# A phase-mixer layer on one core: square addition by DMA, and another order of the first step

## The reference, cut to what matters

```python
def attn(x):                       # x is the layernorm of the input
    omega = einsum('bsd,ed->bse', x, W_omega) + b_omega
    phi = cumsum(omega * exp(log_scale) / sqrt(position), axis=1)
    cm_real, cm_imag = x * cos(phi), x * sin(phi)
    mem_real = cumsum(cm_real, axis=1) / position
    mem_imag = cumsum(cm_imag, axis=1) / position
    ret_real = mem_real * cos(phi) + mem_imag * sin(phi)
    ret_imag = mem_imag * cos(phi) - mem_real * sin(phi)
    context = concatenate([cm_real, cm_imag, ret_real, ret_imag], -1)
    h = gelu(einsum(layernorm(context) * ln_gamma + ln_beta, W1) + b1)
    return x + einsum(h, W2) + b2
x = x + attn(layernorm(x))
x = x + ffn(layernorm(x))          # relu(x @ q(W1).T + b1) @ q(W2).T + b2
# q(W) = clip(round(W / (mean(abs(W)) + 1e-5)), -1, 1): weights of -1, 0 or 1
```

## Time and profile before

| | |
|---|---|
| median of 3 runs | 1533.1 us (1530.54 to 1534.26) |
| the profiled execution's own time | 1533.96 us |
| its span, first to last instruction | 1532.2 us |
| busy: PE, DVE, ACT, POOL | 1470.5, 1438.2, 1253.4, 616.9 us |
| mean granted clock of PE | 0.991 |
| DMA: moved, mean rate | 158.20 MB, 103 GB/s |

### The profile page before, as it was taken

How to read it: one execution, slowest core, us unless ns; L and a number is a source line. 1 busy time by engine, 2 the same in 40 slices (tenths; PEclk the granted TensorE clock), 3 DMA queues, 4 the chain that set the end, 5 groups by cost and what they waited for, 6 DMA issues and landing times.

```text
span 1532.2 us, 29929 instructions
## 1 busy us (share of the span) xinstructions
PE 1470.5 (96%) x10685; PEld 878.0 (57%) x10685; DVE 1438.2 (94%) x2325; ACT 1253.4 (82%) x1773; POOL 616.9 (40%) x393
## 2 busy tenths in 40 slices
PE   3779999999999999999999999999999999999998
PEld 2445566656555665555665655566565566555556
DVE  7999999999999999999999999999999999989954
ACT  6768888888988888988888898888888788888756
POOL 1333444433354443444444334444344444334331
PEclk9899999999999999999999999999999999999999
DMA  6325545555645655654555564455565455555452
GB/s 219 67 58 111 102 80 109 108 111 113 123 76 100 111 104 111 124 107 79 105 111 110 111 125 94 83 111 103 109 125 109 73 109 111 110 111 101 73 90 42
DMA packets 231427, 158.20 MB, mean 103 GB/s; under 512 B 138608, under 2 KB 221552, under 8 KB 231280
## 3 DMA queue, kind: packets, MB, share of 16 engines
q0 software_dynamic: 59376, 83.37, 34.3%
q1 hardware_dynamic: 170272, 69.25, 18.4%
q10 hardware_dynamic: 1632, 3.67, 0.7%
HBM read 24.13 MB, written 33.03 MB: 37 GB/s over the span
## 4 chain that ended last, share of the span: by engine, by line
DVE 35%; PE 24%; issue 14%; ACT 12%; POOL 7%; DMA 4%; SPq 2%; DVEq 1%; ACTq 0%; POOLq 0%
PE ps L966 11%; DVE arena L1332 5%; POOL sqr L535 4%; DVE arena L1400 4%; PE ps L1000 4%; PE ps L987 4%; POOL sqr L537 3%; PE ps L1021 3%; ACT xs L601 3%; DVE mr L1285 3%; ACT base L581 3%; DVE arena L1361 2%; DVE bn L1170 2%; DVE arena L1356 2%; DVE qb L1316 2%
## 5 line engine op out<-in xcount | busy, mean ns | idle before, releaser
L966 PE MATMUL ps<-arena,w_hi 128*128 128x512 f16 x2048 | 609.2, 379 | 3.0 <-DVE arena L1332 1.6
L966 PE MATMUL ps<-arena,w_lo 128*128 128x512 f16 x1024 | 388.3, 379 | 0.0
L966 PEld LDWEIGHTS ps<-arena,w_hi 128*128 128x128 f16 x2048 | 197.5, 98 | 224.2 <-issue 2.0
L987 PE MATMUL ps<-turned,fw_t 128*128 128x512 f16 x1024 | 250.6, 380 | 8.6 <-DMA turned<-rows 4.1
L1000 PE MATMUL ps<-fw_t,arena 128*128 128x256 f16 x2048 | 255.0, 273 | 1.9 <-DVE arena L1400 1.9
L1000 PEld LDWEIGHTS ps<-fw_t,arena 128*128 128x128 f16 x2048 | 197.8, 97 | 63.8 <-issue 16.7
L704 ACT ACTIVATE arena<-ps,relu_bias,relu_scale 128x512 f32<-128x512 f32 x256 | 197.0, 769 | 24.8 <-PE ps L987 24.4
L535 POOL TENSOR_TENSOR sqr<-sqr,turn 128x1024 f32<-128x1024 f32 x32 | 84.3, 2635 | 323.3 <-DVE arena L1332 323.3
L1400 DVE TENSOR_TENSOR arena<-arena 128x512 f16<-128x512 f32 x256 | 172.0, 681 | 19.5 <-ACT arena L713 17.5
L1021 PE MATMUL ps<-w_hi,arena 128*128 128x256 f16 x1024 | 172.9, 273 | 0.3 <-issue 0.3
L966 PEld LDWEIGHTS ps<-arena,w_lo 128*128 128x128 f16 x1024 | 100.0, 98 | 121.0
(11 more groups left out here) (189 smaller groups left out, 2850.4 us busy)
## 6 DMA issues: line engine op xcount, KB each, us to landing
x_rows<-in_L_attn_x SPq DMA_DIRECT2D x32, 512.0 KB, 6.5
rr<-qa POOLq DMA_DIRECT2D x32, 512.0 KB, 6.2
ri<-qb POOLq DMA_DIRECT2D x32, 512.0 KB, 9.0
base<-bias_rows POOLq DMA_DIRECT2D x32, 512.0 KB, 5.5
x<-bias_rows POOLq DMA_DIRECT2D x32, 512.0 KB, 5.5
out<-x SPq DMA_DIRECT2D x31, 512.0 KB, 7.6
out<-x POOLq DMA_DIRECT2D x31, 512.0 KB, 11.2
arena<-in_L_attn_W ACTq DMA_DIRECT2D x1, 2048.0 KB, 11.8
```

The lines of the kernel that those rows point to most:

```text
L966: last = pe.matmul(ps[:, 4 + m], w[:, k, m * P:(m + 1) * P], a[:, c.b, k], start=(i == 0), stop=(i == len(passes) - 1))
L987: last = pe.matmul(ps[:, 4 + m % KE], fw1_t[:, k, m * P:(m + 1) * P], a[:, k], start=(i == 0), stop=(i == len(passes) - 1))
```

## The change

In every step, POOL's L535 becomes an accumulating DMA that no longer waits for `cl_done[3]` (only the addition behind it does), and `output_sum` is issued ahead of `product_imag_sin`. In the first step POOL's `square_lo` comes ahead of `base_bias`; ACT waits for `prepared` behind `whole_turns`; PE waits at its start for the `W1` halves alone; DVE makes `gelu_lo` ahead of the comparisons of `fw2`; PE issues `omega(far)`, two sign groups, `mixer_out`, and the last two sign groups, in this order. The mixer of chunk 0 writes banks 6 and 7, so `hidden` of chunk 1 waits for each `z_done[m]` and, from m = 2 on, for `x1_done`. On DVE the block of scales (L1637 to L1651) moves behind `context_lo` 1 to 3 and the phase scans of chunk 1.

```diff
+        ps_rows_first = ps[:, 6:8, :].rearrange("p b (t d) -> p (b t) d", d=D)
...
+        def mixer_rows(c):
+
+            if c.index == 0:
+                return ps_rows_first
+            return ps_rows_last if c.index == CHUNKS - 1 else ps_rows_b
...
             def step(s):        # POOL
+                if nxt and not now:
+                    square_lo(nxt, ahead)
                 if ahead:
                     base_bias(ahead)
                 if now:
                     inverse_std_2(now)
-                if nxt:
+                if nxt and now:
                     square_lo(nxt, ahead)
...
                     inverse_std_context(nxt)
+                if before:
+                    output_sum(before)
                 if ahead:
                     product_imag_sin(ahead)
                     retrieve(ahead)
-                if before:
-                    output_sum(before)
                 if ahead:
                     square_sums(ahead)
 
             def square_sums(c):
                 need(pool, sqr_done, c)
                 need(pool, sqi_done, c)
+                pool.dma_start(sqr[:, :, :], turn[:, :, :], accum_op=ALU.add).then_inc(q2_done, 16)
+                need_sum(pool, q2_done, c)
                 need(pool, cl_done[3], c)
-                pool.tensor_tensor(sqr[:, :, :], sqr[:, :, :], turn[:, :, :], ALU.add).then_inc(q2_done, 1)
-                need(pool, q2_done, c)
                 pool.tensor_tensor(sqr[:, 0], sqr[:, 0], sqr[:, 1], ALU.add).then_inc(q_done, 1)
...
             def whole_turns(c):        # ACT
                 need(act, y_done, c)
-                need(act, q2_done, c, 1)
+                need_sum(act, q2_done, c, 1)
...
                 if not now:
                     whole_turns(ahead)
+                    prepared(act)
...
                     gelu(nxt, 3)
                     gelu_hi(nxt, 3)
-                    for n in SIGN_GROUPS[4:]:
+                    for n in SIGN_GROUPS[4:6]:
                         group_hi(n)
...
                     relu_hi(now, 7)
+                if nxt and not now:
+                    for n in SIGN_GROUPS[6:]:
+                        group_hi(n)
...
-            prepared(act)
             run(act, step, -1)
...
             def hidden(c, m):        # PE
-                if m < 2:
+                if c.index == 1:
+                    need(pe, z_done[m], c, 1)
+                    if m >= 2:
+                        need(pe, x1_done, c, 1)
+                elif m < 2:
                     need(pe, x1_done, c, 1)
...
-                        for n in SIGN_GROUPS[2:]:
+                        for n in SIGN_GROUPS[2:4]:
                             turn_signs(n)
+                        omega(far)
+                        for n in SIGN_GROUPS[4:6]:
+                            turn_signs(n)
+                        mixer_out(nxt, now)
+                        for n in SIGN_GROUPS[6:]:
+                            turn_signs(n)
+                        return
...
-            prepared(pe)
+            pe.wait_ge(p_lo, len(W1_GROUPS))
             run(pe, step, -1)
...
                 if nxt and not now:        # DVE
+                    for m in range(KE):
+                        gelu_lo(nxt, m)
                     dve.wait_ge(p_fw2, 16)
                     dve.wait_ge(p_tern, 2)
                     signs(1, fw2_in, fw2_signs)
-                    for m in range(KE):
-                        gelu_lo(nxt, m)
...
             first_lo(second)
+            context_lo(first, 1, cmi[:, :, :])
+            context_lo(first, 2, rr[:, :, :])
+            context_lo(first, 3, ri[:, :, :])
+            phase_turns(second)
+            phase_sums(second)
+            carry_phase(second)
             dve.wait_ge(p_spread, 3)
...
             dve.tensor_scalar(thr[:, :], thr[:, :], 0.5, None, ALU.mult).then_inc(p_thr, 1)
-            context_lo(first, 1, cmi[:, :, :])
-            context_lo(first, 2, rr[:, :, :])
-            context_lo(first, 3, ri[:, :, :])
-            phase_turns(second)
-            phase_sums(second)
-            carry_phase(second)
             prepared(dve)
             run(dve, step, -1)
```

More of the change, by code:

```diff
@@ L1016, in mixer_out @@
                     need(pe, csq_done, c)
-                rows = ps_rows_last if c.index == CHUNKS - 1 else ps_rows_b
+                rows = mixer_rows(c)
                 for j in range(NT):
@@ L1367, in mixer_residual @@
                 need_dma(dve, added, c, 2)
-                dve.scalar_tensor_tensor(out=x1[:, c.b], in0=ps_rows_last if c.index == CHUNKS - 1 else ps_rows_b,
+                dve.scalar_tensor_tensor(out=x1[:, c.b], in0=mixer_rows(c),
                                          scalar=h_down[:, 0:1], in1=base[:, c.b], op0=ALU.mult, op1=ALU.add).then_inc(x1_done, 1)
```

## The result

The changed kernel takes 1541.87 us (median of 5 runs, 1538.74 to 1543.89), the kernel before, in the same rounds, 1533.10 (5 runs, 1530.54 to 1537.67). The ratio is 1.006, 95% interval 1.004 to 1.008: slower, where 1518 was forecast. The profiled execution of the changed kernel is its quickest, 1538.74 us with a span of 1536.9.

The account below looks back on a forecast made before the run. PE's 44.85 us of work a step was taken as the floor, with late DVE stretching it to 45.36. Loop -12.9, start -2.3 and end -0.6 sum to -15.8, from 1533.96 to 1518 us; range 1512 to 1531.

Parts of the forecast that it names:

- What bounds the kernel: Steady steps: PE's own work is 44.85 us of a 45.36 us pitch, the rest being waits because DVE is late.
- Square addition by DMA: Every step: replacing POOL's L535 gives DVE back 0.8 to 1.8 us and ACT `q` about 3 us earlier.
- Rival 3: Square addition lands late, 9.0 us after issue; DVE regains only 0.8 us, pitch about 45.1, 1524 us; chance 0.10.
- Output addition ahead of the product: Every step on POOL: `out+=` delays the four `rows2` transposes by 2 us, covered by 2.6 us of slack.
- Rival 1: Output addition holds up the `rows2` transposes, deciding from a landing of 7.7 us on; about 1545 us, chance 0.10.
- Loop sum: 28 steady steps: pitch falls from 45.36 to 44.9 us, 12.9 us gained.
- Start: Preparation and first step, reordered: net -2.3 us, with bounds 0 and -4.5.
- Part (a): Start: scale chain behind the phase scans on DVE; PE's first `hidden` at 61.1 instead of 62.1, -1.0 us.
- Part (b): Start: DVE's 1.3 us earlier `fraction` goes through to `crs`, for which PE waits 1.96 us.
- Part (c): Start: reordered gelu halves, omega, sign groups and mixer; PE idles about 3.5 us for transposes instead of 4.16 for comparisons.
- End: After the loop: PE's 1.6 us wait for a `relu_lo` at 1457 may shrink, -0.6 us.

Follow-up runs that it names:

- e5: The changed kernel with the output addition moved further ahead on POOL, to right behind `square_lo`; 1521.67 us, ratio 0.9936 to before.
- e6: The changed kernel with the output addition cut to the first of its four row blocks, at the same place; 1521.34 us, ratio 0.9937.
- e9: The kernel before with the square addition by DMA and the output addition right behind `square_lo`, old start; 1518.32 us, ratio 0.9916.
- e12: e5 with omega behind the third pair of sign groups on PE and the comparisons ahead of the gelu halves on DVE; 1516.78 us, ratio 0.9907.
- e3: The kernel before with the square addition alone done by DMA; 1524.84 us, ratio 0.9924.
- e4: The kernel before with the changed start alone, both additions as before; 1536.88 us, ratio 1.0020.
- e1: The changed kernel with the output addition back behind the two retrieval additions on POOL; 1528.51 us, ratio 0.9962.
- e10: e5 with the comparisons of the second signs put back ahead of the gelu halves on DVE; 1520.51 us, ratio 0.9931.
- e8: e1 with the first mixer ahead of the third chunk's omega on PE; 1528.48 us, ratio 0.9973.
- e11: e5 with the third chunk's omega behind the third pair of sign groups on PE, DVE order as changed; 1519.20 us, ratio 0.9924.

## Why the prediction was wrong

- **What bounds the kernel: right.** PE's 44.85 us is the floor, and e5, e6, e9 and e12 run on it for 28 steps.
- **Square addition by DMA: right.** It lands after 5.2 us (5.5 taken), the scans take 2.45 us (2.5), ACT's wait is 1.9 us (under 2). Alone it is worth 9.4 us of medians in e3, with the better place of `out+=` 11.5 in e9. Rival 3 was sized right, by its own mechanism.
- **Output addition ahead of the product: the step that failed.** It reads: "The delay that it gives them lies between nothing and its whole landing alone, 6.1 us; I take 2, since both only share the DMA engines, and the slack covers that." The value between the two bounds had no row behind it, and the slack of 2.6 us (24.9 for PE's need less 22.3 for the last landing, both from the residual) wasn't there either. e5, which is the changed kernel without the collision, shows it: over the 28 steps of the loop the last transpose lands 23.1 to 24.6 us after the residual, 23.5 at the median, and PE turns to `ffn_in` at 25.4 in every step. So the slack is 1.9 us at the median and 0.7 at the least. The first issue is 0.7 us later than forecast (16.7, not 16.0), the four issues take 5.5 us, not 5.1, and PE's need is 0.5 us later than in the one step that the prediction took. In the changed kernel the last transpose lands at 25.1 to 27.6, 25.9 at the median: a delay of 2.4 us at the median and about 4 at the most. Part of it is the issue of the four, 6.7 us at the median. So 2 was near the median and failed all the same, as the delay has a wide spread and the slack was thinner. Where `out+=` took 8.5 us (issued at 395.1), a transpose took up to 8.3 and PE waited 2.1. The median landing of `out+=` is 6.8 us, near the 6.1 that I took; so its own speed isn't what was misjudged.
- **Rival 1 came true**, at 1541.87 where 1545 stood, with a chance of 0.10 that was too low. Its limit, a landing of 7.7 us, was wrong: it has the transposes complete when the addition is. In the 28 steps the last of them landed 0.8 to 2.9 us behind `out+=`, 1.3 at the median, so that PE waited in 16 steps though `out+=` took over 7.7 us in three. That the time came near 1545 is luck in part: many small waits, not a few by that limit. What I held against it, that 11.2 us is measured behind `ri` and 6.1 is nearer, was right and of no help.
- **Loop sum: -12.9 forecast, right for the kernel with this step mended.** From the first to the last residual (31 steps), before takes 1392.6 us (109.0 to 1501.6), e5 1379.0, e9 1378.5, the changed kernel 1398.7. That is about -14 for the mechanism, and +20 for the collision. Of the 18.8 us that the 28 steps lose (45.52 against 44.85), the waits view has 14.4; where the rest goes stays open.
- **Start: -2.3 forecast, +2.6 (e4) to +3.7 (e1 less e3) measured.** Part (a) has the right sign: PE's first `hidden` starts at 60.94, where 61.1 was said, but at 61.0 to 62.0 in the other eight profiles with this start, against 61.9 to 62.2 with the old one. Part (b) holds: PE's wait for `crs`, 1.96 us at the old L952, is down to 0.6. Part (c) failed: I put the landing of chunk 2's transposes at 95.0 and PE's idle time at 3.5 us. In the six profiles with the changed place of omega, PE's wait for `turned<-xs` and the first residual are 6.5 and 107.7 (the changed kernel), 6.7 and 108.9 (e10), 8.0 and 110.1 (e5), 8.5 and 111.6 (e1), 9.8 and 114.1 (e4), 9.9 and 113.4 (e6). The changed kernel, e1, e5 and e6 have the same code up to there, so 3.4 us of wait and 5.7 of residual are what executions differ by. The quickest of them is the changed kernel's profile, which looks as if the start had gained. There the four transposes are issued early enough, from 86.94 on, but the fourth, at 90.89, lands after 5.9 us, where it took 3.3 before, beside the addition to `rr` issued 0.23 us behind it. In e6 it takes 9.2 us. I had also not counted ACT behind the sign groups, and set the comparisons' 4.16 us as saved, where PE waits 6.8 us for them in e8 and e11 and 4.2 in e12, 2.6 more for the gelu halves ahead of them. The `hidden` of chunk 1, for which 106 to 107 was said, starts at 107.93, and at 105.68 in e12.
- **End: -0.6 forecast, nothing measured.** From the last residual to the end it is 30.6 us before (1532.2 - 1501.6) and 30.5 after; PE's 1.6 us wait for a `relu_lo` is still there in e5 and e12.

What makes that fourth transpose late goes together with one thing in the profiles. The queue that the page calls instruction (q8) moves a packet of 16 KB near it. In the nine profiles in which this starts between 0.3 us ahead of the fourth issue and 0.8 us behind it, the landing takes 5.6 to 9.2 us; where it starts 0.9 and 1.0 us behind (e3, e9), 3.8 and 4.4; where it starts more than 8 us later (before, e8, e12), 3.3. No run moves this packet alone, so it isn't shown to be the cause.

The Trainium skill, "DMA: Bandwidth & Descriptors", Queues, rings and completion order, was cited for the rival: a completion increment lands only after every earlier write of its DMA engine. The trace agrees as far as it goes, since the three transposes issued beside `out+=` landed after it, and over the 28 steps 84 of the 85 issued behind it did (the one other landed 0.17 us ahead of it). The same section says that each DMA engine takes the queues with work in turn, a whole packet at a time. The rows agree with it in part: from 628 to 629 us it is 147 packets to 147, by bytes 0.15 MB to 0.04, but from 626 to 627 it is 87 to 5. This second rule should have moved the chance, since by equal turns the queue with the smaller packets gets the smaller part of the bytes. That packet size is what delays them is argued; no run changed it.

## What to carry to other kernels

A transfer that is moved must be laid against every other transfer of its new window, and above all against those that a full engine waits for; between "nothing" and "its whole landing" take the far end unless a row of the trace shows the two side by side. Read the slack from many steps, and as its least value, not from one step. Look for the gap that it fits in whole: here the same DMA costs 20 us when it is issued 17.5 us behind the residual, and nothing at 8.8. And an order in which an engine waits for a late landing also holds up every engine that follows the work queued behind it; undo such orders together, as each may hide the other. A first step that differs by 5.7 us between executions of the same code is judged by medians, not by one profile.

The version with both, e12, is the best: 1516.78 us, 0.9907 of before (0.9888 to 0.9926).

## What the runs showed of the hardware

- A 512 KB accumulating DMA beside four transposes: they landed after 4.8 us instead of 2.5 (medians), and their issue on SP took 6.69 us instead of 5.12. Cut to 128 KB (it then lands after 3.2 us), 2.6.
- An accumulating DMA between two SBUF tiles, 512 KB, lands after 5.2 us (4.5 to 6.7) where it follows `ri` in its queue and after 8.9 where `out+=` is put between.
- The longer PE waits for omega in the first step, the lower its granted clock is afterwards. The mean between 90 and 110 us is 0.66 in e4 and e6 (waits for omega of 9.8 and 9.9 us), 0.74 in e5 and e1 (8.0 and 8.5) and 0.83 in the changed kernel and e10 (6.5 and 6.7), where 0.50 is 1.2 GHz. From the start of omega to the first residual it takes 10.9 us in the last two and 11.5 to 12.1 in the other four. So the longer waits cost 0.6 to 1.2 us beyond their length.
- Two DVE scans of 128x512 f32 take 2.45 us, 3.4 with POOL's 128x512 addition beside them (e3) and 4.3 with its 128x1024 addition ahead of that the earlier trace rows.
